# One head's product with the attention weights, and the last rows of the output projection: products with the high halves first, those with the low halves last, behind a wait of their own

## The reference

```
x = x + layernorm(attention(layernorm(x)))      # 32 heads of 128, RMS norm of q and k over all heads
x = x + layernorm(ffn(layernorm(x)))            # x W_base + gated low-rank experts (8 x rank 16)
attention: scores = q k^T / sqrt(128); p = softmax(scores); out = p v; result = out Wo + bo
```

## Time and profile before

| what | value |
|---|---|
| median of three runs | 1071.59 us (1071.46 to 1071.72) |
| the profiled execution, first to last instruction (its span) | 1069.7 us |
| busy: TensorE, weight loads, VectorE, ScalarE, GpSimd | 98%, 53%, 74%, 69%, 64% |
| mean granted TensorE clock over the span | 0.998 |
| chain that ended last, share of TensorE | 91% |

### The profile page before, as it was taken

The page is one execution under the profiler, slowest core; times in us unless marked ns, Lnnn a source line. Parts: engine busy times, 40 slices in busy tenths (PEclk is TensorE's granted clock), DMA queues, the critical chain, the costliest instruction groups (busy, mean ns, idle before and its releaser), DMA issues.

```text
span 1069.7 us, 20038 instructions
## 1 busy us (share of the span) xinstructions
PE 1052.9 (98%) x5781; PEld 563.7 (53%) x5781; DVE 789.6 (74%) x1831; ACT 741.3 (69%) x1470; POOL 681.1 (64%) x597
## 2 busy tenths in 40 slices
PE   7999999999999999999999999999999999999997
PEld 4444444444445655555555555555555555555454
DVE  8767766666645887777777777777777777778887
ACT  4666766666656787676777767677776767777756
POOL 2667767676657476676666667666666766666713
PEclk9999999999999999999999999999999999999999
DMA  6688985656663679977676776767677676765702
GB/s 240 175 237 261 269 232 194 223 215 222 203 142 135 199 187 267 227 173 177 177 184 165 189 179 165 176 178 187 162 190 179 163 176 180 189 163 128 175 33 79
DMA packets 312072, 197.76 MB, mean 185 GB/s; under 512 B 275424, under 2 KB 279392, under 8 KB 312032
## 3 DMA queue, kind: packets, MB, share of 16 engines
q1 hardware_dynamic: 304400, 193.71, 65.5%
q10 hardware_dynamic: 7632, 3.57, 1.5%
HBM read 94.45 MB, written 35.68 MB: 122 GB/s over the span
## 4 chain that ended last, share of the span: by engine, by line
PE 91%; DVE 5%; ACT 2%; DMA 1%; issue 1%; SPq 0%; POOL 0%; DVEq 0%; ACTq 0%
PE ps L1236 30%; PE ps L1237 30%; PE ps L1238 30%; DMA wa_stage<-w_qk 1%; DVE pair_q L2061 1%; ACT ps L1031 0%; DVE ps L2047 0%; DVE stats L1630 0%; DMA pair_k<-pair_q 0%; ACT xh L1024 0%; ACT pair_q L1040 0%; PE ps L1348 0%; DVE y L2011 0%; DVE wa_lo L1735 0%; DVE y L2172 0%
## 5 line engine op out<-in xcount | busy, mean ns | idle before, releaser
L2047 DVE TENSOR_SCALAR_CACHE_REDUCE ps<-ps,score_down 128x512 f32<-128x512 f32 x256 | 177.5, 756 | 88.6 <-PE ps L1238 87.9
L2061 DVE SCALAR_TENSOR_TENSOR pair_q<-ps,row_inv,pair_q 128x512 f16<-128x512 f32 x256 | 174.5, 744 | 54.7 <-ACT pair_q L1040 54.6
L1031 ACT ACTIVATE ps<-ps,neg_max 128x512 f32<-128x512 f32 x256 | 168.2, 657 | 44.9 <-DVE ps L2047 44.9
L1236 PE MATMUL ps<-xh,wa_hi 128*128 128x512 f16 x512 | 194.3, 379 | 1.8 <-DVE wa_lo L1735 1.8
L1237 PE MATMUL ps<-xl,wa_hi 128*128 128x512 f16 x512 | 194.3, 379 | 0.0
L1238 PE MATMUL ps<-xh,wa_lo 128*128 128x512 f16 x512 | 194.3, 379 | 0.0
L1040 ACT ACTIVATE pair_q<-ps,row_inv 128x512 f16<-128x512 f32 x256 | 154.9, 688 | 21.5 <-DVE row_inv L2054 21.5
L758 POOL CAST oth<-o_t 128x512 f16<-128x512 f32 x62 | 37.8, 609 | 201.0 <-ACT o_t L1005 200.9
L664 POOL TENSOR_TENSOR acc<-acc,squares 128x512 f32<-128x512 f32 x120 | 151.1, 1281 | 1.7 <-ACT squares L882 1.7
L1237 PE MATMUL ps<-wv_lo,xh 128*128 128x256 f16 x512 | 139.7, 273 | 0.0
L1236 PE MATMUL ps<-wv_hi,xh 128*128 128x256 f16 x512 | 139.7, 273 | 0.0
(11 more groups left out here) (236 smaller groups left out, 2220.9 us busy)
## 6 DMA issues: line engine op xcount, KB each, us to landing
q_k_scratch<-qk_out SPq DMA_DIRECT2D x64, 512.0 KB, 3.9
qk_in<-q_k_scratch SPq DMA_DIRECT2D x64, 512.0 KB, 3.4
wa_stage<-w_qk SPq DMA_DIRECT2D x32, 512.0 KB, 4.8
u_stage<-w_vo SPq DMA_DIRECT2D x32, 512.0 KB, 5.5
wv_stage<-w_vo SPq DMA_DIRECT2D x16, 512.0 KB, 4.2
wo_stage<-w_vo SPq DMA_DIRECT2D x16, 512.0 KB, 4.4
qk_tops<-qk_top_scratch ACTq DMA_DIRECT2D x27, 128.0 KB, 4.2
y<-x SPq DMA_DIRECT2D x8, 256.0 KB, 5.4
```

Source lines behind the costliest of these rows:

```text
L1031: act.activation(ps[:, SCORE + i, :], ps[:, SCORE + i, :], ACT.Exp, bias=neg_max[:, sl, i:i + 1], scale=-1.0, accum_out=row_sum[:, sl, i:i ...
L1236: pe.matmul(outp, lhs[0], rhs[0], start=first, stop=False)
L2047: dve.tensor_scalar(ps[:, SCORE + i, :], ps[:, SCORE + i, :], score_down[:, sl, i:i + 1], None, ALU.mult, ALU.min, accum_out=neg_max[:, sl ...
L2061: dve.scalar_tensor_tensor(out=pair_q[:, 1, i, :], in0=ps[:, SCORE + i, :], scalar=row_inv[:, sl, i:i + 1], in1=pair_q[:, 0, i, :], op0=AL ...
```

## The change

`attend` is written in two halves: behind `high_turned` the eight products with the turned high halves (`vh` and `vl` for each of four tiles), then the wait for `low_turned`, then four products of `vh` with the turned low halves. This holds for all 64 attendings; the last one, which had this order already, now calls `attend`. `last_rows` gets the same form: for each head eight products of `oth` behind `last_high_ready`, then four of `otl` behind `last_low_ready`. The number and the kinds of products stay what they were.

```diff
             def attend(n, sl, b, bank=OB):
+                d = slice(sl * P, (sl + 1) * P)
                 pe.wait_ge(high_turned, 16 * n + 16)
+                for k in range(TB):
+                    for v in (vh, vl):
+                        pe.matmul(ps[:, bank, :], v[:, TB * b + k, d], pair_k[:, sl, 0, :, k, :],
+                                  start=k == 0 and v is vh, stop=False)
                 pe.wait_ge(low_turned, 16 * n + 16)
-                d = slice(sl * P, (sl + 1) * P)
                 for k in range(TB):
-                    ins = three(ps[:, bank, :], (vh[:, TB * b + k, d], vl[:, TB * b + k, d]),
-                                (pair_k[:, sl, 0, :, k, :], pair_k[:, sl, 1, :, k, :]), k == 0, k == TB - 1)
+                    ins = pe.matmul(ps[:, bank, :], vh[:, TB * b + k, d], pair_k[:, sl, 1, :, k, :],
+                                    start=False, stop=k == TB - 1)
                 ins.then_inc(o_product, 1)
...
-            pe.wait_ge(high_turned, 16 * N + 32)
-            for k in range(TB):
-                for v in (vh, vl):
-                    pe.matmul(ps[:, VB, :], v[:, TB + k, P:2 * P], pair_k[:, 1, 0, :, k, :],
-                              start=k == 0 and v is vh, stop=False)
-            pe.wait_ge(low_turned, 16 * N + 32)
-            for k in range(TB):
-                ins = pe.matmul(ps[:, VB, :], vh[:, TB + k, P:2 * P], pair_k[:, 1, 1, :, k, :],
-                                start=False, stop=k == TB - 1)
-            ins.then_inc(o_product, 1)
+            attend(N + 1, 1, 1, VB)
 
             def last_rows(h):
 
+
+                pe.wait_ge(last_high_ready, h + 1)
                 for t in range(TB):
                     cols = slice((TB + t) * P, (TB + t + 1) * P)
-                    ins = three(ps[:, SCORE + t, :], (oth[:, h, cols], otl[:, h, cols]),
-                                (wo_hi[:, 1, h, :], wo_lo[:, 1, h, :]), h == 0, h == 1)
+                    for w in (wo_hi, wo_lo):
+                        pe.matmul(ps[:, SCORE + t, :], oth[:, h, cols], w[:, 1, h, :],
+                                  start=h == 0 and w is wo_hi, stop=False)
+                pe.wait_ge(last_low_ready, h + 1)
+                for t in range(TB):
+                    cols = slice((TB + t) * P, (TB + t + 1) * P)
+                    ins = pe.matmul(ps[:, SCORE + t, :], otl[:, h, cols], wo_hi[:, 1, h, :], start=False, stop=h == 1)
                     if h == 1:
                         ins.then_inc(y_product, 1)
 
-            pe.wait_ge(last_low_ready, 1)
-
             pe.wait_ge(y_added, 2 * N - 1)
             last_rows(0)
-            pe.wait_ge(last_low_ready, 2)
             last_rows(1)
             in_between(OB, 6)
```

## The result

The changed kernel takes 1073.61 us (median of 21 runs, 1073.05 to 1074.90); the kernel before, run beside it, 1072.09 us (21 runs). The ratio is 1.0015, 95% interval 1.0008 to 1.0021: 0.9 to 2.3 us slower. I had forecast 1071.4, 0.15 under the kernel before. The sign is wrong, and the time lies outside my range of 1070.3 to 1072.6; it is still within the 0.2% that I had called no change, a class to which I had given 0.91, but it got there by a way that none of my cases had: that the class holds is luck.

A forecast was written before the change was run, and what follows sets the result against it. TensorE, busy 98% of the span, was taken as the bound, except from 1017 us on. Span 1069.7 - 0.24 (third attending) + 0.09 (last rows) = 1069.55; the median, 1.9 above, gives 1071.4 us, range 1070.3 to 1072.6.

The forecast's parts named there:

- The third attending: Near 388 us: the 0.97 us stall for the turning DMA goes, 0.24 of it is kept: -0.24 us.
- a wait for VectorE's addition: First rows item of step 4, writing the same bank as the addition: a short new wait, about 0.7 us.
- its own delay of 0.14: Time from the end of VectorE's addition to TensorE's first rows item of step 4, taken like the release at 388.05.
- The wait in mid-attending: The low-halves wait moved to the ninth product in the 64 attendings: 0 us, at most 3.2.
- Rival 4: Each wait in mid-attending costs 0.05 us, 3.2 us in all: 1074.6 us, slower; chance 0.03.
- The last rows: After the last attending: TensorE done 0.72 us earlier, but VectorE gets tile 4 later: +0.09 us.
- Idle time before turning z: After the last rows TensorE sits idle 1.3 us instead of 0.47 before turning z.
- The clock: After the longer idle time before turning z TensorE stays at 2.4 GHz: 0 us.
- Rival 3: The clock falls before z is turned, in 1023.85 to 1025.13, costing 2.7 us: 1074.1 us, slower; chance 0.04.
- Rivals 1 and 2: Third attending: 0.97 us kept in full, 1070.7, chance 0.15; or no gain, high halves landing with low, 1071.7, chance 0.18.
- The 0.97: Delay in us of TensorE's first product at the third attending, waiting for the turning DMA in the kernel before.

The follow-up runs named there:

- e5: Changed kernel with 56 more semaphore instructions (7 lots of 8) in TensorE's program ahead of the attending; 1072.22 us, ratio 0.9995 to the kernel before.
- e2: Kernel before with only the last rows changed, attend as before; 1071.99 us, ratio 0.9992 to the kernel before.
- e7: Changed kernel with a lone semaphore instruction before each attending's high products and head 1 of the last rows tile by tile; 1071.65 us, ratio 0.9988.
- e3: Changed kernel with one lone semaphore instruction between the wait for the high halves and the first product of each attending; 1072.03 us, ratio 0.9996.
- e8: Changed kernel with one more semaphore instruction behind the products of each attending; 1073.78 us, ratio 1.0011 to the kernel before.
- e6: Kernel before with 56 more semaphore instructions in TensorE's program ahead of the attending; 1072.09 us, ratio 0.9993.
- e4: Kernel before with 24 more semaphore instructions in TensorE's program, in lots of 6 ahead of the attention; 1071.80 us, ratio 0.9995.
- e9: Kernel before with 28 more semaphore instructions (7 lots of 4) in TensorE's program ahead of the attending; 1072.12 us, ratio 0.9996.
- e10: Kernel before with 35 more semaphore instructions (7 lots of 5) in TensorE's program ahead of the attending; 1072.06 us, ratio 0.9990.

## Why the prediction was wrong

**The third attending: the step that failed.** I wrote: "The low halves' DMA is issued at 383.98 and takes 3.93 us, so it lands at 387.91", and of the ninth product "the low halves are there since 387.91. The stall goes". I took the landing as fixed, since the change touches no DMA. It isn't: the change took away the stop of TensorE's queue ahead of the attending, the next piece of code was fetched 3.4 us sooner against the work (387.26 instead of 389.56 + 1.14), and that fetch held the transfer up by 1.67 us, so that it landed 5.60 us after its issue. The term that I had at -0.24 came out at **+1.59**.

Of the rest of this step the working was right, and e5 shows it with the landing where I had put it: first product 0.22 behind the item, no wait for a DMA, then a wait for VectorE's addition (0.57 in its timeline, I had said "about 0.7"), and 30.80 - 31.04 = **-0.24**, the figure of the forecast (which by its own delay of 0.14 should have been 0.23).

I also left out the edge by which the loss came. I checked that the low halves had 0.90 us to spare for the ninth product (388.81 - 387.91). VectorE's `low_halves` of the next head waits for the same landing, and started at 388.18, 0.27 behind it. TensorE alone would have lost nothing against the kernel before: its last product of this attending starts at 390.77 + 3 x 0.216 = 391.42, before it was 388.05 + 11 x 0.216 + 1.14 = 391.57. All of the +1.59 runs over VectorE. `low_halves` starts 1.50 later (390.82 against 388.18 + 1.14). The maxima and the addition start 1.82 later, since the small operation on score_down between them took 0.68 instead of 0.35 too; why is not shown. The rows item starts 1.59 later, since it now starts 0.14 behind the end of the addition and before 0.37 (395.48 to 395.85).

**Was there a sign of it?** Yes. Line 566, the issue of the low halves' DMA, over the whole trace of the kernel before:

```profile
DMA to landing us min/median/max: 3.8/3.9/5.6
```

A transfer whose price I put at 3.93 takes 5.6 at times, and the prediction neither says at which times nor bounds the term with it.

**The wait in mid-attending: right.** From attending 4 to the last product of attending 64 the changed kernel needs 618.54 us, before 618.55. Rival 4 (3.2 us) is out.

**The last rows: right.** Forecast +0.09, measured +0.10 (52.82 against 52.72, and in e2 alone 0.11). Idle time before turning z: forecast 1.3, measured 1.30.

**The clock: right.** Behind the idle 1.30 us the products of z keep their pace, and the stretch behind the last attending is longer by the 0.10 alone. Rival 3 (+2.7) is out. The granted clock is 1.00 from 1026 to 1032. The rule of the Trainium skill (TensorE: Matmul & The Clock Gate, Part 1) that I had set against the change isn't borne out by this idle stretch of 1.30 us. The clock did fall elsewhere in this profile, from 8.22 to 11.63, after TensorE had been idle for 2.05 us up to 8.07, and in e7 from 12.04 on, after an idle stretch of 2.50 us up to 10.63. In the other eleven profiles no fall is recorded before TensorE's last product, though the kernel before has an idle stretch of 1.82 us. The price of rival 3 rested on the spacing of the products at the start alone: the granted clock recorded for 0 to 7 us is 1.00.

**Rivals 1 and 2.** The 0.97 was not kept in any kernel (e5: 0.24), and the high halves were ahead, as the rows had said: they landed at 387.36, the first product started at 388.22. None of my cases had a transfer that the change itself makes slower; the chance of 0.07 for slower stood for other mechanisms.

**What stays open.** That the place of the lone instruction moves the fetch is shown by e3 and e8. The point at which the queue asks for code isn't. In the changed kernel the fetch starts at 387.26, 0.10 before the high halves have landed (383.33 + 4.03 = 387.36), so a wait that rides on a product doesn't hold it. And behind the end of the stop the fetch starts after 1.6 us in the kernel before, but after 3.8 in e3. In both it is nearer to TensorE's next lone semaphore instruction, the one ahead of the next scores, which ended at 389.02 and 389.45: 0.54 and 1.08 us before the fetch. Nor do the records show why a fetch of 16 KB halts the other queue for 1.4 us. And a fetch inside the third attending's low transfer with the old order was tried and not reached; late turnings in the old order are shown only at other places (e6, and 454 to 456).

The Trainium skill (Runtime: NRT & Kernel Launch, Instruction fetch mechanics) says that an engine's code is refilled in blocks of 16 KiB by the sequencer's own DMA queue while it executes, at a cost that is mostly hidden. The trace agrees with the size, 16,384 bytes on q8; of the 18 pieces in the changed kernel I found one that cost time, and there it was 1.8 us against e5 (32.63 and 30.80), 1.6 against the kernel before.

## What to carry to other kernels

Before a transfer's latency is used as a constant, look at its largest value in the trace and at what stood beside it; then ask every engine that waits for the landing, not only the one under study, how much it has to spare. A change in an engine's waits can change where its queue stops, and with it when its next code is fetched, as it did here: where the time of a change is off by one or two us at a single place, look at the instruction queues there. Shifting the code by some harmless instructions, with the work unchanged (e5), tells such an effect from one of the change itself. It takes more than one count: 24 more moved nothing at the place looked at (e4), and 28 more brought a loss of their own (e9).

## What the hardware showed that I had not expected

- A piece of 16,384 bytes on the instruction queue q8 that starts 1.3 to 3.27 us behind the issue of a turning DMA makes it land after 5.2 to 5.9 us instead of 3.9, in 34 of 34 cases; in the changed kernel the DMA engines move 0 to 10 GB/s for about 1.4 us meanwhile. A piece of 8,192 bytes on q14 at the same place goes with a landing after 4.5 in the median (52 cases).
- A fetch at the issue of such a DMA made the issue itself longer: 2.33 us on SP's queue instead of 1.67 (e9), 2.28 in e10.
- One lone semaphore instruction in front of eight products, costing nothing itself, moved a fetch by 3.5 us against the first attending (22.70 us behind its first product in e3, 19.23 in e8) and the kernel by 1.8 us.
